# Two transformer layers on one core: a new order for the first batch, the last router, the tiles' results and the dense products

## The reference

```python
xn = _layernorm(x)
x = x + attention0(xn) + fp4_ffn(xn)        # 16 heads of 8; fp4: silu(gate) * up, then down
xn = _layernorm(x)
x = x + attention1(xn) + moe(xn)

def fp4_quant_dequant(x):                    # blocks of 16 along the last dim
    scale = jnp.maximum(jnp.max(jnp.abs(xb), -1, keepdims=True) / 6.0, 1e-12)
    idx = jnp.searchsorted(_MID, jnp.abs(xb / scale))
    return _GRID[idx] * jnp.sign(xb) * scale

def moe(xf):
    gates = softmax(relu(xf @ Wr1 + br1) @ Wr2 + br2)
    tg, ti = top_k(gates, 2); tg = softmax(tg / 2)
    out = silu(xf @ Ws1 + bs1) @ Ws2 + bs2
    for e in range(8):
        h = silu(xf @ We1[e] + be1[e]) @ We2[e] + be2[e]
        out = out + jnp.sum(tg * (ti == e), -1)[:, None] * h
    return out
```

## Time and profile before

| | us |
|---|---|
| median of 3 runs | 1525.27 |
| lowest and highest | 1523.20, 1525.59 |
| the profiled execution | 1524.82 |
| its span, first to last instruction | 1522.9 |
| PE, DVE, ACT, POOL busy | 1218.8, 974.3, 777.5, 384.6 |
| granted TensorE clock, mean | 0.913 |

### The profile page before, as it was taken

The page is one execution under the profiler, slowest core; times in us unless marked ns, Lnnn a source line. Parts: engine busy times, 40 slices in busy tenths (PEclk is TensorE's granted clock), DMA queues, the critical chain, the costliest instruction groups (busy, mean ns, idle before and its releaser), DMA issues.

```text
span 1522.9 us, 19413 instructions
## 1 busy us (share of the span) xinstructions
PE 1218.8 (80%) x6739; PEld 517.1 (34%) x6807; DVE 974.3 (64%) x1651; ACT 777.5 (51%) x979; POOL 384.6 (25%) x373
## 2 busy tenths in 40 slices
PE   2568678878887888788878887888789947888885
PEld 1113223323332333233313331333124225677741
DVE  7764877677777767777677767767785264422323
ACT  1146146655665556556655665566565812233354
POOL 6032314121413041204121413041112221244430
PEclk9769579999999999989999999999999968999997
DMA  5329563115312521253116312531230083355544
GB/s 142 71 94 338 205 159 108 33 53 142 108 33 73 150 80 32 79 132 92 32 47 151 106 32 67 130 100 33 84 76 15 13 210 89 119 169 168 169 145 125
DMA packets 151938, 160.08 MB, mean 105 GB/s; under 512 B 14073, under 2 KB 140226, under 8 KB 151842
## 3 DMA queue, kind: packets, MB, share of 16 engines
q1 hardware_dynamic: 141746, 131.89, 32.3%
q10 hardware_dynamic: 5552, 17.58, 3.0%
q0 software_dynamic: 4544, 9.38, 1.9%
HBM read 90.19 MB, written 68.09 MB: 104 GB/s over the span
## 4 chain that ended last, share of the span: by engine, by line
PE 51%; DVE 18%; ACT 11%; DVEq 8%; issue 5%; DMA 3%; SPq 2%; POOL 1%; ACTq 0%; POOLq 0%
PE sums L358 11%; PE mx L370 10%; ACT ex L713 7%; DVE nm L1022 7%; PE mx L339 5%; PE ring L469 4%; PE mx L460 3%; PE ring L269 2%; PE ring L264 2%; PE ring L444 2%; PE ring L274 2%; ACT L713 2%; DVEq L997 2%; PE mx L420 2%; PE ring L327 1%
## 5 line engine op out<-in xcount | busy, mean ns | idle before, releaser
L713 ACT ACTIVATE ex<-mx 128x1024 f32<-128x1024 f32 x512 | 516.0, 1024 | 391.4 <-PE mx L370 389.6
L1022 DVE TENSOR_REDUCE nm<-mx 128x2 f32<-128x1024 f32 x512 | 614.5, 1217 | 125.4 <-PE mx L339 124.8
L370 PE MATMUL mx<-qs,ks 74*128 74x512 bf16 (+1 forms) x956 | 308.9, 406 | 81.7 <-DVE nm L1022 69.9
L358 PE MATMUL sums<-ex,vs 128*18 128x512 f32 x2048 | 287.7, 635 | 6.8 <-ACT pv_sb L717 4.5
L339 PE MATMUL mx<-km,qm 32*128 32x512 bf16 x1024 | 209.9, 422 | 42.0 <-DVE nm L1022 25.7
L370 PEld LDWEIGHTS mx<-qs,ks 128*128 128x128 bf16 (+1 forms) x1024 | 63.1, 99 | 371.4 <-issue 187.1
L339 PEld LDWEIGHTS mx<-km,qm 32*128 32x128 bf16 x1024 | 47.9, 92 | 236.9 <-issue 132.2
L1435 POOL TENSOR_TENSOR parts<-qk_f,parts 128x512 bf16<-128x512 f32 x32 | 36.4, 1158 | 325.8 <-DVE parts L929 325.8
L1444 POOL TENSOR_TENSOR h_sb<-h_sb,binade 128x704 f32<-128x704 f32 x32 | 53.5, 1673 | 185.2 <-DVE binade L964 184.0
L1406 POOL TENSOR_TENSOR rstd<-veps,minus_half 128x4 f32<-128x4 f32 x16 | 16.6, 1040 | 286.5 <-DVE veps L914 286.4
L1463 POOL DMA_INDIRECT xsort<-xn,pos_i x64 | 62.7, 980 | 87.9 <-DVE pos_i L1109 70.8
(11 more groups left out here) (210 smaller groups left out, 1544.5 us busy)
## 6 DMA issues: line engine op xcount, KB each, us to landing
scratch<-parts SPq DMA_DIRECT2D x128, 256.0 KB, 3.6
xsort<-hs ACTq DMA_DIRECT2D x32, 520.0 KB, 4.7
ks<-scratch SPq DMA_DIRECT2D x64, 256.0 KB
qs<-scratch SPq DMA_DIRECT2D x64, 256.0 KB
qs<-wmoe SPq DMA_DIRECT2D x20, 514.0 KB, 3.6
ks<-wmoe SPq DMA_DIRECT2D x19, 514.0 KB, 3.5
qm<-scratch SPq DMA_DIRECT2D x64, 128.0 KB, 2.6
km<-scratch SPq DMA_DIRECT2D x64, 128.0 KB, 2.7
```

What stands on the lines that cost most here:

```text
L358: done = pe.matmul(acc[32 * j:32 * j + 2 * VW, :], values[:, start:start + 2 * VW], ex[:, s % NEX, j, :], start=q == 0 and t == 0, stop=q ...
L370: done = pe.matmul(bank[:, j, :], ks[l][r, h, t * P:(t + 1) * P], qs[l][r, h, :], start=True, stop=True)
L713: act.activation(ex[:, s % NEX, 2 * i:2 * i + 2, :], bank[:, :, :], ACT.Exp, scale=SCALE).then_inc(free, 1)
L1022: dve.tensor_reduce(nm[l][:, t, h:h + 2], bank[:, :, :], AX.X, ALU.max, negate=True).then_inc(free, 1)
```

## The change

The first batch: only ten units of maxima (`FIRST_UNITS`) run in the prologue; the other six run in slots 0 to 5 of `turn_a(0)`, the first eight units of batch 1 in its slots 8 to 15, and the last eight in slots 0 to 7 of `turn_b(0)`. The norm, projections and split of batch 1 move from `turn_a(0)` into the prologue. The weights are rounded by GpSimd in place of VectorE, x is quantized ahead of the second and third weight, and up's and down's weights are turned between units. SP's list follows, and `load_max` waits group by group. GpSimd sets the constants of layer 1 later.

All turns: v products move from (1,b) to (3,b) and (5,b), `norm1` to (8,a), and a new place "d" behind the flushed sums takes gate, up and the shared expert's first products. The last batch's router, ranks, places and table of tiles come earlier. The tiles' results go to a pair bank. The last batch is combined before its last projection, and its result is stored behind that projection.

```diff
+FIRST_UNITS = 10
...
+        def fp4_binade(n):
+            return ex[:, 0, n, 0:fp4_piece(n).shape[1]]
+
+        def units_a(b, k):
+
+            if b >= 1:
+                return [(1, b - 1, k)]
+            if k < SLOTS - FIRST_UNITS:
+                return [(0, 0, FIRST_UNITS + k)]
+            return [(0, 1, k - 8)] if k >= 8 else []
+
+        def units_b(b, k):
+            if b == 0:
+                return [(0, 1, 8 + k)] if k < 8 else []
+            return [(0, b + 1, k)] if b < LAST else []
...
-                bank = to_ring(("TO", i))
+                bank, full = to_pair(("TO", i))
...
-                    if at == (1, "a"):
+                    if at == (1 if b else 6, "a"):
                         max_rows(0, b, 1)
...
-                if b + 1 <= LAST:
+                if 1 <= b < LAST:
                     if at == (0, "b"):
                         norm0(b + 1)
...
-                    if at == (1, "b"):
+                    if at == (5, "b"):
                         v1(b - 1)
...
-                    if at == (7, "b"):
+                    if at == (7, "d"):
                         shared_hidden(b - 1, 0)
-                    if at == (8, "b"):
+                    if at == (8, "d"):
                         shared_hidden(b - 1, 1)
...
-                if at == (9, "b"):
+                if at == (8, "a"):
                     norm1(b)
-                if at == (10, "a"):
+                if at == (10 if b < LAST else 9, "a"):
                     q1(b)
-                if at == (10, "b"):
+                if at == ((10, "b") if b < LAST else (10, "a")):
                     k1(b)
...
-                    if at == (1, "b"):
+                    if at == (3, "b"):
                         v0(b + 1)
-                    if at == (6, "b"):
+                    if at == (6, "d"):
                         gate_pair(b + 1, 0)
-                    if at == (7, "b"):
+                    if at == (7, "d"):
                         gate_pair(b + 1, 1)
-                    if at == (8, "b"):
+                    if at == (8, "d"):
                         up_pair(b + 1, 0)
-                    if at == (11, "b"):
+                    if at == (11, "d"):
                         up_pair(b + 1, 1)
...
+                    if at == (8, "b"):
+                        router_hidden(b)
+                    if at == (9, "b"):
+                        router_logits(b)
                     if at == (11, "a"):
-                        router_hidden(b)
-                    if at == (12, "a"):
-                        router_logits(b)
-                    if at == (14, "a"):
                         ranks(b)
-                    if at == (15, "b"):
+                    if at == (13, "b"):
                         gates_transposed(b)
...
+            gate_weights("wg", 0)
             quantized_x(0)
-            for u in range(SLOTS):
+            for u in range(FIRST_UNITS):
+                if u == 1:
+                    norm0(1)
                 if u == 2:
-                    ring_read(pe, "wd")
                     gate_pair(0, 0)
+                if u == 3:
                     gate_pair(0, 1)
+                    q0(1)
                 if u == 4:
+                    k0(1)
+                if u == 5:
+                    gate_weights("wu", 1)
+                if u == 6:
+                    ring_read(pe, "wu")
                     up_pair(0, 0)
-                if u == 6:
+                if u == 7:
+                    down_weights()
+                if u == 8:
                     up_pair(0, 1)
-                if u == 10:
+                if u == 9:
                     max_rows(0, 0, 0)
...
-                    if at == (12, "a"):
+                    if at == (9, "b"):
                         router_sort(b)
+                    if at == (10, "a"):
                         router_choice(b)
                         router_hits(b)
-                    if at == (13, "a"):
+                    if at == (11, "a"):
                         gate_difference(b)
-                    if at == (14, "b"):
+                    if at == (11, "b"):
                         places(b)
-                    if at == (14, "c"):
+                        tile_table()
+                    if at == (12, "a"):
                         router_weights(b)
-                        tile_table()
...
-            for b in range(LAST):
+            for b in range(B):
                 combine(b)
             sums_divided(1, LAST, 0)
             sums_divided(1, LAST, 2)
             add_projection(1, LAST)
-            combine(LAST)
...
-            third_part(0, 0)
-            pool.wait_ge(p3_ready, 1)
-            set_ones(1)
             pool.wait_ge(weights_in, 16 * N_WEIGHT_DMAS)
             residual0(0)
+            round_weights(0)
+            third_part(0, 0)
             round_x(0)
+            normalize(0, 1)
+            residual0(1)
+            round_weights(1)
+            round_weights(2)
+            third_part(0, 1)
+            pool.wait_ge(p3_ready, 2)
+            set_ones(1)
             round_h(0, 0)
...
+            load_x(1)
             store_early(0, 0)
             load_max(0, 0)
             store_late(0, 0)
             sp.wait_ge(ones_set, 4)
             load_stacks(0, 0, 0)
             load_stacks(0, 0, 1)
-            load_x(1)
-            sp.wait_ge(ones_set, 8)
+            load_x(2)
+            store_early(0, 1)
+            load_max(0, 1, [0])
             load_rows(0, 0, 0)
+            load_max(0, 1, [1])
+            store_late(0, 1)
+            load_max(0, 1, [2, 3])
+            load_rows(0, 0, 1)
```

More of the change, by code:

```diff
@@ L151, in two_layers @@
         amax, qrs = sb("amax", [P, 2 * F0 // QB]), sb("qrs", [P, 2 * F0 // QB])
-        qsc = [sb("qsc0", [P, 2 * F0 // QB]), sb("qsc1", [P, 2 * F0 // QB])]
+        qsc = [sb(f"qsc{i}", [P, 2 * F0 // QB]) for i in range(4)]
         hs = sb("hs", [P, EC, T])
@@ L573, in turn_a @@
                     work_a(b, k, "a")
-                    if b >= 1:
-                        maxima(1, b - 1, k, 0)
+                    for unit in units_a(b, k):
+                        maxima(*unit, 0)
                     if b <= LAST:
@@ L578, in turn_a @@
                     work_a(b, k, "b")
-                    if b >= 1:
-                        maxima(1, b - 1, k, 1)
+                    for unit in units_a(b, k):
+                        maxima(*unit, 1)
                     flush_sums()
+                    work_a(b, k, "d")
                     if b <= LAST:
@@ L593, in turn_b @@
                     work_b(b, k, "a")
-                    if b + 1 <= LAST:
-                        maxima(0, b + 1, k, 0)
+                    for unit in units_b(b, k):
+                        maxima(*unit, 0)
                     if b >= 1:
@@ L598, in turn_b @@
                     work_b(b, k, "b")
-                    if b + 1 <= LAST:
-                        maxima(0, b + 1, k, 1)
+                    for unit in units_b(b, k):
+                        maxima(*unit, 1)
                     flush_sums()
+                    work_b(b, k, "d")
                     if b >= 1:
@@ L613, in tile_step, with gate_weights, down_weights @@
                     tile_out(i - 1)
+            def gate_weights(name, n):
+                pe.wait_ge(fp4_done, n + 1)
+                bank = to_ring(name)
+                for c, (f, m) in enumerate(FC):
+                    done = pe.transpose(bank[:, f:f + m], work[0:m, (3 * n + c) * P:(3 * n + c + 1) * P], ident[0:m, 0:m])
+                done.then_inc(ring_full, 1)
+            def down_weights():
+                pe.wait_ge(fp4_done, 3)
+                bank = to_ring("wd")
+                for c, (f, m) in enumerate(FC):
+                    done = pe.transpose(bank[0:m, c * P:(c + 1) * P], work[:, 6 * P + f:6 * P + f + m], ident[:, :])
+                done.then_inc(ring_full, 1)
             pe.wait_ge(consts_set, 6)
@@ L797, in work_b @@
                     sums_out(0, b, 1)
[L798 to L799 removed]
+                if b + 1 <= LAST and at == (3, "b"):
+                    values0(b + 1)
                 if at == (4, "a"):
@@ L862, in _ @@
             values0(0)
-            for name, dst in (("wg", wgT), ("wu", wuT)):
-                copy_out(name, dst[:, :], width=F0)
+            copy_out("wg", wgT[:, :], width=F0)
+            copy_out(("xqT", 0), xqT[:, :])
+            copy_out(("xT0", 1), xnT[0][:, :])
+            gates(0, 0)
+            gates(0, 1)
+            qk_out(0, 1, 0)
+            qk_out(0, 1, 1)
+            copy_out("wu", wuT[:, :], width=F0)
             bank = from_ring("wd")
@@ L1360, in _ @@
             split_third()
-            dve.drain()
-            quantize_weights(1)
-            dve.drain()
-            quantize_weights(2)
             for step in range(4):
                 quantize_x(0, step)
-            for u in range(SLOTS):
-                if u == 4:
+            norm_stats(0, 1)
+            norm_moments(0, 1)
```

(9 more changed lines are left out.)

163 lines of the change are left out of this document (78 added, 85 removed).

## The result

| | before | changed |
|---|---|---|
| median | 1525.43 us (4 runs) | 1565.43 us (4 runs) |
| ratio to before, 95% interval | | 1.0267 (1.0233 to 1.0302) |
| profiled execution, its span | 1524.82, 1522.9 | 1558.35, 1556.2 |
| granted clock, mean | 0.913 | 0.878 |

The change makes the kernel 40 us slower; I had forecast 14 us faster. The changed kernel's profiled execution was the shortest of its four, 7 us under their median, so its trace shows 33 of the 40 us. First its chain by engine, against the earlier trace rows.

The account below looks back on a forecast made before the run. It took the bound to change from stage to stage (chain 51% TensorE), ordinary turns near TensorE's limit. Parts -11.3 + 2 + 6.6 - 9.7 - 1.6 = -14.0 took 1524.8 to 1511 us; forecast 1503 to 1520 (55%), whole range 1494 to 1526.

Parts of the forecast that it names:

- 1 to 3, first turn: Start and turns a and b of batch 0: -17.7 + 12.4 - 6 = -11.3 us.
- 4, v: Ordinary turns: v leaving slot 1 saves part of its 1.11 us wait for the ring bank, -5.7 us.
- 4, norm 1: Second-kind turns: the norm's transposes leaving slot 9 gain 0.8 us in each of 6 turns, -4.8 us.
- 4, products: Ordinary turns: late shared products cost 0.9 us in each of two slots in 7 turns, +12.6 us; gate slots nothing.
- 5, router: Last batch: the table of tiles delays the layer-1 split and the next turn's first maxima, +6.6 us (0 to +8).
- 6, tiles' results: Tiles: no wait for the ring bank's copy, 4.17 us a tile for 4.53; net -9.7 us (-17 to -3).
- 7, end: Program end: the last combine leaves the end but delays the last sums' division by 0.8 us; -1.6 us.
- part 4: Ordinary turns: moving v, the norm's transposes and the products, net +2 us (-15 to +12).
- Late products: Rival, ordinary turns: all 14 shared and 12 gate slots pay the full 1.44 us, 37.4 for 12.6; 1536 us, 10%.
- Part 3: Turn b of batch 0: loses 8 units of maxima; next turn starts 6 us earlier (0 to 12).
- the first turn gives nothing: Rival, turn a of batch 0: full of TensorE work, units may cost what they saved; 1522 us, no change, 15%.
- table rule: Rival, ordinary turns: about 1.38 us of drain behind each table load makes late products free; 1498 us, 6%.

Follow-up runs that it names:

- e8: e5 with the last turn's router, and q and k there, put back as before the change; the fastest kernel: 1486.4 us, ratio 0.9733.
- e5: Changed kernel with the products and v back in their old places, norm 1 left at its new place (8,a): 1491.5 us, ratio 0.9776.
- e11: e8 with the tiles' results put back from a pair bank to the ring bank: 1506.1 us, ratio 0.9895.
- e12: The kernel before with only the new first turn; norm 1, last router, tiles' results and end as before: 1522.3 us, ratio 0.9996.
- e1: Changed kernel with only the gate, up and shared expert's first products put back, v still late: 1530.2 us, ratio 1.0021.
- e3: Changed kernel with products, v and the ordinary turns' norm 1 put back in their old places: 1509.4 us, ratio 0.9895.
- e2: Changed kernel with only the two v products and their copies put back to slot 1, products still late: 1528.6 us, ratio 1.0035.
- e10: e8 with the last batch's combination and store put back behind the last projection: 1493.9 us, ratio 0.9787.
- e4: e1 with the second maxima pair of slot 1 computed five times over, 8 more matmuls a turn: 1510.2 us, ratio 0.9865.
- e7: e5 with only the shared expert's first products put late, behind the second weighted sums of slots 7 and 8: 1515.3 us, ratio 0.9934.
- e9: e5 with only the table of tiles put back to the end of slot 14, behind the split's third part: 1496.6 us, ratio 0.9821.
- e13: e7 with ScalarE's silu of the shared products one exponential later, behind the next slot's first exponential: 1543.2 us, ratio 1.0127.

## Why the prediction was wrong

Measured pairs beside my terms (medians, each uncertain by 5 to 9 us; e8 against e5 and e11 are across groups):

| part | forecast | measured | from |
|---|---|---|---|
| 1 to 3, first turn | -11.3 | -0.2 | e12, before |
| 4, v | -5.7 | +38.7 | e1, e5 |
| 4, norm 1 | -4.8 | -17.9 | e5, e3 |
| 4, products | +12.6 | +37.1 | e2, e5 |
| 5, router | +6.6 | +5.1 | e5, e8 |
| 6, tiles' results | -9.7 | -19.7 | e8, e11 |
| 7, end | -1.6 | between -1.7 and 0 | traces of e8, e10 |
| sum | -14 | +43 | changed: +40 |

**The step that failed is part 4**: it priced every move at full clock, and it had v's move wrong besides.

For v, I took the earlier trace rows as a wait that could only shrink, and asked only what VectorE would do. I did not ask what else slot 1 waits for: its sums need ScalarE's copy of the sums (L717 of before), which the product had covered. So at full clock nothing was gained: about +2 us where I had -5.7. The other 36 us of its 38.7 came through the clock, and e4 got 20 of them back by filling the idle stretch.

For the products, the full-clock price was right. I had 0.9 us for each of 14 shared slots, 12.6 us, and nothing for gate and up; measured at full clock it is 1.0 and 0.7 us in slots 7 and 8, 12 us, and nothing. What I had left out is the other 25 of the 37.1 us, which stand in slots at half clock. Late products was one of my rivals, at 10% and 1536 us, but with 1.44 us as the most a slot could pay: in the changed kernel slots 7 and 8 take up to 9.7 and 8.6 us, for 7.0 and 6.3, and the silu's waits of 1.92 and 2.81 us are longer than 1.44.

That the clock is what was missing follows from these lengths. Beside e5, e1 has 84 us more at half clock and e2 79; and the same slot with the same work takes about 1.6 us more with 3.4 us of half clock in it (in e7 slot 8 takes 8.6 us for 6.98). Why a late product or a late v brings the half clock is less sure: for v, e4 shows that the idle stretch brings much of it (58 of the 84 us go when it is filled); for the products no run filled it.

The norm gained three times my term. What I had put down came: slot 9 of second-kind turns takes 4.6 us for 5.5, 5 us in six turns. The rest I had not seen. Slot 0 of the following first-kind turn starts 0.9 us sooner and takes 3.1 us for 5.3: in e3 it is at half clock in all six turns, in e5 in none. That it was good for 13 us beyond the forecast is luck, as far as the forecast goes.

**Parts 1 to 3**: the first exponential was right (73.7 for 75). Turn a of batch 0 is 64.7 us where I said 60; many of its slots take 4.9 us, not 3.1, and these are at half clock (granted clock 0.72 over the turn); I had 3 us for that. Part 3 moved the wrong thing: the exponentials came 17.6 us earlier, but what the turn needs is the maxima's operands, and the maxima start only 9.8 us earlier (188.61 for 198.41). By the end of turn a of batch 1, 3.7 us of it are left in the changed kernel's trace and 6.9 in e12's, and none in e12's median. The rival "the first turn gives nothing" came out, and the half clock and that wait are what its trace shows for it; whether the zeroing transfers that it named delayed the stores, no run tested.

**Part 5** was right in place (the rows of e5 and e9) and near in size (4.5 to 5.1 us for 6.6), though e9, which put the table alone back, gained nothing in total. **Part 6** had the right mechanism and too small a size: the last 28 steps save 11.4 us, with late loads and all, where I had 9.4 less 2.5; the steps beside the maxima gained 5 us and not 2, and the rest lies ahead of the first step and behind the last. **Part 7**: the division comes 6 us later behind the last exponential and not 0.8, because the chain of combinations starts with the last tile and had become longer than the scores. In the changed kernel my -1.6 was therefore more likely about +4 (the estimate above).

The table rule of the Trainium skill ("ScalarE: Activation LUTs", "What ACT_TABLE_LOAD costs"), by which late products would be free, did not come out: late products were not free, the silus in the rows above follow the product, and where the product is early they follow the load by 0.02 us, as in the earlier trace rows.

## What to carry to other kernels

A wait that a product hides is not seen in the profile: before moving work out of a slot, list every semaphore that the rest of the slot waits for, with the time it is set. Where TensorE is the limit of a stage for most of its time, price a move also by the granted clock behind it: here a stretch of 1.4 us without TensorE work cost far more than itself. To tell the two apart, compare the same slot in turns with and without half clock. And where a result shares bank pairs with the main loop, look at both ends, when it is made and when it is read; here moving either end lengthened the loop.

## What the runs showed of the hardware

Behind short idle stretches on TensorE, as that of 1.39 us in e1, the granted clock fell from 1.0 to 0.5 (2.4 to 1.2 GHz): the sums then take 1.91 us for 1.05, the shared product 3.43 for 1.98. The stretches at half clock in these turns of e1 last from 3.4 to 20.5 us. In the sixteen kernels, whose matmuls are nearly the same, the time at half clock in the fourteen turns ran from 101 to 249 us; the fastest had the least and the slowest the most. It is not steady: two kernels alike up to the tiles (e8 and e10) differed by 20 us of it and 6 us of time. Apart from it the turns are steady to 0.1 us a slot. From batch 1 on, slot 10 of the first-kind turns was at half clock in all sixteen kernels (5.0 us), in every turn but one, of e13, and there it took 3.1 us. What decides where it falls stays open; filling an idle stretch lowered it (201 to 143 us), the same matmuls in a slot that still had v came with more (101 to 154).
